# First-layer attention on TensorE: the transposes of unit i-2 issued ahead of the scores of unit i

## What is computed

```python
x_norm = _group_norm(x, gn_scale, gn_bias).reshape(b, seq, c)
qkv = x_norm @ w_qkv + b_qkv
q, k, v = jnp.split(qkv, 3, axis=-1)
scale = 1.0 / math.sqrt(HEAD_DIM)
q, k, v = (to_heads(q), to_heads(k), to_heads(v))
weight = jnp.einsum('bhld,bhsd->bhls', q * scale, k * scale)
weight = jax.nn.softmax(weight, axis=-1)
out = jnp.einsum('bhls,bhsd->bhld', weight, v)
out = out.transpose(0, 2, 1, 3).reshape(b, seq, c)
out = out @ w_out + b_out
return (x_flat + out).reshape(b, h, w, c)
```

## Time and profile before

| | |
|---|---|
| median of 3 runs | 4412.85 us (4411.47 to 4413.67) |
| the profiled execution | 4408.6 us, of which the span from first to last instruction is 4406.9 us |
| TensorE matmuls busy | 4119.7 us, 93% |
| VectorE busy | 3071.6 us, 70% |
| ScalarE busy | 2523.8 us, 57% |
| GpSimd busy | 1313.1 us, 30% |
| mean granted TensorE clock | 0.975 of full speed |
| first layer's attention, 8 stretches | of some 181 us each, the first one from 102 to 284 us |

### The profile page before, as it was taken

The page is one execution under the profiler, slowest core; times in us unless marked ns, Lnnn a source line. Parts: engine busy times, 40 slices in busy tenths (PEclk is TensorE's granted clock), DMA queues, the critical chain, the costliest instruction groups (busy, mean ns, idle before and its releaser), DMA issues. The chain is left out here.

```text
span 4406.9 us, 65281 instructions
## 1 busy us (share of the span) xinstructions
PE 4119.7 (93%) x22762; PEld 3415.9 (78%) x22762; DVE 3071.6 (70%) x5125; ACT 2523.8 (57%) x5486; POOL 1313.1 (30%) x1423
## 2 busy tenths in 40 slices
PE   7999989989999999899999899999999898989998
PEld 6977978978878879789788577777777776767777
DVE  3983965947839839659478368677686867676867
ACT  3864845837828638558377146464646363645545
POOL 1432423422324314234234004041323223140404
PEclk9999999999999999999999899999999999999999
DMA  2221221221212212212211302030303121212212
GB/s 79 49 66 32 55 64 28 58 59 29 68 39 46 66 35 49 70 28 58 58 39 39 118 23 84 26 86 15 96 20 78 39 58 58 58 58 48 68 33 64
DMA packets 113184, 236.20 MB, mean 54 GB/s; under 512 B 17260, under 2 KB 33704, under 8 KB 112808
## 3 DMA queue, kind: packets, MB, share of 16 engines
q1 hardware_dynamic: 112808, 231.41, 19.6%
HBM read 80.35 MB, written 33.55 MB: 26 GB/s over the span
## 5 line engine op out<-in xcount | busy, mean ns | idle before, releaser
L560 DVE TENSOR_REDUCE a_neg_max<-a_ps 128x1 f32<-128x1024 f32 x512 | 626.2, 1224 | 396.3 <-PE a_ps L443 396.3
L577 DVE TENSOR_TENSOR a_pl<-a_ps,a_ph 128x512 fp32r<-128x512 f32 x1024 | 655.0, 680 | 11.6 <-ACT a_ph L519 8.3
L519 ACT ACTIVATE a_ph<-a_ps 128x512 fp32r<-128x512 f32 x1024 | 555.1, 593 | 188.2 <-PE a_ps L454 185.1
L526 ACT ACTIVATE a_prob<-a_ps,a_neg_max 128x1024 f32<-128x1024 f32 x512 | 572.7, 1118 | 20.5 <-DVE a_neg_max L560 20.5
L1562 POOL TENSOR_SCALAR b_prob<-b_prob,b_row_inv 128x256 f32<-128x256 f32 x512 | 247.6, 484 | 1049.2 <-DVE b_row_inv L1480 1013.3
L427 PE MATMUL a_ps<-a_ph,a_v 128*128 128x256 f32 x2048 | 550.7, 302 | 0.0
L640 POOL TENSOR_TENSOR a_qk<-a_fold_s,a_fold_r 64x256 f32<-64x256 f32 x256 | 188.4, 736 | 1213.1 <-DVE a_fold_s L568 1213.1
L454 PE MATMUL a_ps<-a_ident,a_prob 128*128 128x128 f32 x4096 | 534.4, 273 | 10.0 <-DVE a_pl L577 10.0
L454 PEld LDWEIGHTS a_ps<-a_ident,a_prob 128*128 128x128 f32 x4096 | 474.9, 140 | 86.9 <-issue 19.3
L427 PE MATMUL a_ps<-a_pl,a_v 128*128 128x256 f32 x2048 | 509.3, 282 | 0.0
L442 PE MATMUL a_ps<-a_kh,a_qs 128*128 128x512 f32 x1024 | 410.4, 401 | 31.2 <-ACT a_prob L526 13.0
(11 more groups left out here) (246 smaller groups left out, 9340.7 us busy)
## 6 DMA issues: line engine op xcount, KB each, us to landing
a_qs<-a_qk SPq DMA_DIRECT2D x128, 256.0 KB, 4.3
a_kl<-a_qk SPq DMA_DIRECT2D x128, 256.0 KB, 4.4
a_xtok<-in_x SPq DMA_DIRECT2D x64, 256.0 KB, 4.4
a_tok<-in_x SPq DMA_DIRECT2D x64, 256.0 KB, 4.4
x<-a_tok SPq DMA_DIRECT2D x64, 256.0 KB, 2.0
b_xs<-x SPq DMA_DIRECT2D x64, 256.0 KB, 4.9
b_qs<-b_qh SPq DMA_DIRECT2D x64, 256.0 KB, 3.0
b_qs<-b_ql SPq DMA_DIRECT2D x64, 256.0 KB, 3.8
```

Of the source, the lines that this page charges most:

```text
L519: act.activation(ph[:, b % 2, 4 * g:4 * g + 4, (u % 2) * P:(u % 2 + 1) * P], ps[:, 4 + n % 2, :].rearrange("p (k q) -> p k q", k=4), ACT.C ...
L526: act.activation(prob[:, i_ % 2, :], ps[:, 2 * (i_ % 2):2 * (i_ % 2) + 2, :] .rearrange("p a b -> p (a b)"), ACT.Exp, bias=neg_max[:, i_:i ...
L560: dve.tensor_reduce(neg_max[:, i_:i_ + 1], ps[:, 2 * (i_ % 2):2 * (i_ % 2) + 2, :] .rearrange("p a b -> p (a b)"), AX, ALU.max, negate=Tru ...
L577: dve.tensor_tensor(pl[here], ps[:, 4 + n % 2, :].rearrange("p (k q) -> p k q", k=4), raw(ph[here]), ALU.subtract).then_inc(pl_ok, 1)
```

## The change

In each step of TensorE's loop the block that transposes unit i-2 moves from behind the scores of unit i to ahead of them. Nothing is added or removed; every wait keeps its count; the other engines' loops are the same.

```diff
@@ -428,6 +428,18 @@
                                                        start=kt == 0 and e == 0, stop=kt == TT - 1 and e == 1)
                                 if part == 1:
                                     mm.then_inc(av_ps, 1)
+                        if 2 <= i_ < U + 2:
+                            u = i_ - 2
+                            pe.wait_ge(exp_ok, u + 1)
+                            for g in range(2):
+                                n = 2 * u + g
+                                if n >= 2:
+                                    pe.wait_ge(pl_ok, n - 1)
+                                for kk in range(4):
+                                    kt = 4 * g + kk
+                                    mm = pe.transpose(ps[:, 4 + n % 2, kk * P:(kk + 1) * P],
+                                                      prob[:, u % 2, kt * P:(kt + 1) * P], ident[:])
+                                mm.then_inc(tr_ps, 1)
                         if i_ < U:
                             h, t = i_ // TT, i_ % TT
                             j = h % 2
@@ -442,18 +454,6 @@
                                 pe.matmul(bank, q_, kl[:, j, n], start=False, stop=True)
                             mm.then_inc(score, 1)
-                        if 2 <= i_ < U + 2:
...
-                                mm.then_inc(tr_ps, 1)
                         if i_ == U + 2:
                             turn(range(4))
```

## The result

| | before | after |
|---|---|---|
| median, runs side by side | 4412.16 us | 5106.49 us (5101.11 to 5109.73) |
| ratio | | 1.1574, 95% interval 1.1554 to 1.1594 |
| profiled execution | 4408.6 us | 5105.75 us |
| span | 4406.9 us | 5104.0 us |

One slow execution of the kernel before (14895.74 us, beside the first four experiments) is left out of every comparison; the medians of that kernel beside the different runs lie between 4409.7 and 4413.4 us, so a difference of a few us between runs says nothing.

A forecast was written before the change was run, and what follows sets the result against it. TensorE sets the pace, VectorE close behind. The ring's 262.2 us plus 0.8 at the head, less 176.8 now, makes 86.2 us an image, 689 for eight; 4412.85 + 689 = 5102 us, range 5045 to 5175.

The forecast's parts named there:

- The closed ring: First layer's attention: scores, maximum, split, transposes, scores; 2.40 us to the transposes plus 1.69 to the next scores, 4.09 a turn.
- The turns: Steps of the first layer's attention: 4.09 us without a fold, 4.42 with one in even heads, 4.66 in odd heads.
- S(2): Start of the last scores matmul of unit 2 in an image; forecast at 107.01 us instead of 106.24, 0.8 later.
- S(63): Start of the last scores matmul of unit 63, 61 turns behind that of unit 2; stretch forecast at 262.2 us.
- AV runs beside the ring: TensorE in the first layer's attention: AV's 1.04 us falls into the pause before the transposes and adds nothing.
- The tail behind S(63): End of each image's attention: costs nothing, as the 2.40 us chain to the transposes is the same before and after.
- The clock: TensorE's granted clock in the attention: stays full despite a pause near 1 us in each turn; nothing charged.
- rival (a): First layer's attention: pauses make the clock swing; some 5510 us with half of it at the low level, all 5930; chance 0.08.
- a granted clock under 1.00 in the attention: Listed sign that the forecast is wrong, pointing to TensorE's clock swinging between its two levels.
- Rival (b): First layer's attention: a longer link through ScalarE, which writes `ph` before VectorE's split; 0.2 us a turn gives 5200 us; chance 0.06.
- Rival (c): Faster: transposes placed ahead cover TensorE's wait for a new head's staged operands, 22 us in all, 4391 us; chance 0.01.
- The forecast of TensorE's wait for the split: Transposes waiting for `pl` should rise from some 10 us over the kernel to about 700 us.

## Why the prediction was right, step by step

**The closed ring** was the whole of it. The key was one row of the kernel before: at the tail, where no scores follow, the chain from scores to transposes could be read at its full length, 2.40 us, against the 2.99 that the old order gave it and the 1.27 that the new one gives. It measured 2.40 in the changed kernel. What had been 0.59 us of room became a pause in every turn.

**The turns** were right to 0.01 us: 4.09, 4.42 and 4.67 (366.18 to 370.85 in the timeline) against 4.09, 4.42 and 4.66. The count too: from S(2) at 107.56 to S(63) at 370.85 it is 263.3 us in the first image where 262.2 was forecast; 0.7 of the difference is the clock's fall in two turns, below, and in the seventh image, where it did not fall, it is 262.6. That AV runs beside the ring was confirmed twice: moved into it, it cost its length; filled up with 0.7 us of useless work, the pause cost nothing. The tail behind S(63) stayed at 2.40 (370.85 to 373.25).

**The clock** is where the forecast was incomplete. It said full clock in the attention, and in the steady part that held. At the head of seven of the eight images it did not. Steps 2 to 4 have no AV yet, so the pauses in front of the transposes are 1.6, 2.0 and 2.0 us, and the clock fell behind one of the two longer ones; in the seventh image the same pauses left it full. In the timeline of TensorE in the first image:

```profile
114.05 1.16 PE L440 MATMUL a_ps<-a_ident,a_prob 128*128 128x128 f32 x8 [2.00 <-DVE a_pl L577]
114.97 0.60 PE L454 MATMUL a_ps<-a_kh,a_qs 128*128 128x512 f32 x1
115.36 0.63 PE L455 MATMUL a_ps<-a_kl,a_qs 128*128 128x512 f32 x1
```

And in stretches, before and in the fall:

```profile
110.00:114.00 4.00, 2.04 (x12) 1.41 (x12) 2.33 (x4) 2.25 (x5) 0.00 (x0) 1.00 0.00 2
114.00:118.00 4.00, 3.95 (x19) 3.38 (x20) 1.69 (x3) 1.68 (x4) 0.00 (x0) 0.65 0.00 0
```

The scores start 0.43 us apart there instead of 0.23. With filler the head keeps its clock (1.00 from 100 to 120 us, against 0.91). The price stands in the trace: what the eight images take from S(2) to S(63) beyond 262.6 us adds up to 7 us. The medians fit it (a loss of 694.3 us without and 689.9 with filler), though 4 us are under what they can tell for sure. This was rival (a), at a small part of its price; by the forecast's own list, a granted clock under 1.00 in the attention was a sign of being wrong, and at the heads it occurred.

That 689 us forecast and 694 measured (697 by the spans) lie so close is in a small part luck. The term for the clock was put at nothing and is 7 us; turns and heads at full clock come to 86.7 us an image instead of 86.2, 4 us in all; and outside the eight stretches, where nothing was forecast, the profiled kernel takes 3 us less.

**Rival (b)**, a longer link through ScalarE, did not occur: `ph` waits for the transposes, and in the two turns shown above it was done 1.3 us ahead of the split with the fold copies before it (202.89, split at 204.23) and 1.5 us ahead without them (206.84, split at 208.32). It needs VectorE's order turned as well to become the bound. **Rival (c)** was priced right (21 us for 22, measured by staging earlier and not by moving the transposes) and its condition was not met. TensorE's busy time was said to hardly move and rose by 3%. The forecast of TensorE's wait for the split, about 700 us, came out as 604 (443.0 + 161.1): TensorE's busy time rose from 4119.7 to 4241.1 us, since a matmul in front of a pause counts its way through the array and the wait of the second group hides inside the transposes' row.

## What to carry to other kernels

Before an instruction with a wait is moved forward in an in-order queue, look for the chain from the last instruction now in front of it to what it waits for; if what it is moved past is the start of that chain, the move closes a ring, and the ring's length, not the engines' work, becomes the step. Such a chain can be read at full length where the loop starts or ends and the cover is missing. A wait that costs nothing in the trace (here 1.3 us an image) says nothing of its room: that is the distance between what is needed and what is given, 0.59 us here.

## What the runs showed of the hardware

When TensorE makes short, regular pauses, its granted clock can fall. It then changes between its two levels, 2.4 and 1.2 GHz; the mean over the stretch from 200 to 250 us, with one pause in nearly every turn (at full clock; the shortest without a fold, the longest with one):

| kernel | pause before the transposes, us | granted clock |
|---|---|---|
| changed, with filler | 0.3 to 0.6 | 1.00 |
| half of AV, with filler | 0.7 to 1.1 | 1.00 |
| transposes ahead of AV, with filler | 0.7 to 1.3 | 1.00 |
| changed | 1.1 to 1.4 | 1.00 |
| VectorE's order turned too | 1.2 to 1.9 | 0.93 |
| half of AV | 1.5 to 1.9 | 0.91 |
| transposes ahead of AV | 2.0 to 2.6 | 0.80 |

The fillers, put into the pauses, gave the last two kernels their full clock back. They shorten the pause and add work to the turn at once; which of the two holds the clock is not told apart by these runs. Nor does a pause of a given length always do the same: pauses of 2.0 us at an image's head lowered the clock in seven of eight images of the changed kernel.

The Trainium skill's page "TensorE: Matmul & The Clock Gate" says in "A second HAM failure mode: psum-queue depth-cycling" that frequent short idling between groups of matmuls can make the clock swing. The three lower rows agree with it; the changed kernel, with pauses in every turn too, does not show it outside the images' heads.

What had not been expected is the consequence: leaving out 0.48 us of work in a step made the kernel 98 us slower, and 1.2 us of useless work in a step made another one 624 us faster. An experiment that leaves out work must therefore be read with its clock.
